# Two cross-attention and feed-forward layers on one core: values of a pair of head groups by seven products, and a written-out order at the end

## What is computed

```python
x = x + _L0_xattn_ref(_layernorm(x), ctx, mask, position_bias, ln_weight, w_q, w_k, w_v, w_out)
x = x + _L0_ffn_ref(_layernorm(x), ...)      # 512x512 base, low-rank part of 4 experts, softmax routing
x = x + _L1_xattn_ref(_layernorm(x), ctx, Wq, bq, Wk, bk)    # one head of width 512, values = ctx
x = x + _L1_ffn_ref(_layernorm(x), qweight, scale, zero_point, bias)   # 512x512, 6 bit codes

# _L0_xattn_ref
x = _rmsnorm(hidden_states, ln_weight)
h_q, h_k, h_v = x @ w_q.T, kv @ w_k.T, kv @ w_v.T            # each 1024 x 4096
score = softmax(where(mask, einsum(h_q, h_k) + position_bias))
out = einsum(score, h_v) @ w_out.T + hidden_states
```

## Time and profile before

| | |
|---|---|
| median of 3 runs | 980.95 us (980.33 to 982.57) |
| the profiled execution | 981.03 us, of which 979.2 us from first to last instruction |
| busy, of the span | PE 98%, PE weight loads 85%, DVE 62%, POOL 48%, ACT 40% |
| mean granted clock of TensorE | 0.993 of full |
| DMA | 169.6 MB, mean 173 GB/s |

### The profile page before, as it was taken

The page is one execution under the profiler, slowest core; times in us unless marked ns, Lnnn a source line. Parts: engine busy times, 40 slices in busy tenths (PEclk is TensorE's granted clock), DMA queues, the critical chain, the costliest instruction groups (busy, mean ns, idle before and its releaser), DMA issues.

```text
span 979.2 us, 16713 instructions
## 1 busy us (share of the span) xinstructions
PE 956.6 (98%) x5645; PEld 835.3 (85%) x5645; DVE 605.7 (62%) x1124; ACT 393.7 (40%) x1100; POOL 469.4 (48%) x527
## 2 busy tenths in 40 slices
PE   9999999999999999999999999999999999999995
PEld 7888888888888888888888888888888888777773
DVE  5664774656566666666565656565656568376774
ACT  5654444333434243433333333434333333424652
POOL 3550735464645545545546455555464612113676
PEclk9999999999999999999999999999999999899998
DMA  9223537747474756555555647474747442301001
GB/s 334 92 90 131 166 136 237 254 156 268 156 277 159 263 172 240 188 213 196 212 210 195 239 170 258 158 260 171 262 171 261 152 152 88 118 1 26 19 22 54
DMA packets 58185, 169.60 MB, mean 173 GB/s; under 512 B 5767, under 2 KB 7947, under 8 KB 57884
## 3 DMA queue, kind: packets, MB, share of 16 engines
q1 hardware_dynamic: 58140, 169.01, 49.1%
HBM read 158.51 MB, written 10.49 MB: 173 GB/s over the span
## 4 chain that ended last, share of the span: by engine, by line
PE 90%; DVE 4%; POOL 2%; ACT 2%; issue 1%; DMA 1%; SPq 0%; ACTq 0%; POOLq 0%; DVEq 0%
PE ps_q L326 6%; PE ps_q L328 6%; PE ps_q L327 6%; PE ps_v L328 6%; PE ps_v L326 6%; PE ps_v L327 6%; PE ps_o L326 6%; PE ps_o L328 6%; PE ps_o L327 6%; PE ps_s L1760 6%; PE ps_t L1787 6%; PE ps_k L326 6%; PE ps_k L328 5%; PE ps_k L327 5%; PE ps_t L1777 3%
## 5 line engine op out<-in xcount | busy, mean ns | idle before, releaser
L1206 DVE TENSOR_TENSOR acc<-ps_o,acc 128x512 f32<-128x512 f32 x128 | 87.9, 686 | 154.0 <-PE ps_o L328 154.0
L653 ACT ACTIVATE scores<-scores,neg_max 128x128 f32<-128x128 f32 x256 | 99.8, 391 | 197.0 <-DVE neg_max L1287 197.0
L326 PE MATMUL ps_v<-wv_hi,ct_hi 128*128 128x256 f32 x504 | 142.7, 283 | 0.0
L328 PE MATMUL ps_v<-wv_hi,ct_lo 128*128 128x256 f32 x504 | 142.7, 283 | 0.0
L327 PE MATMUL ps_v<-wv_lo,ct_hi 128*128 128x256 f32 x504 | 142.6, 283 | 0.0
L951 POOL TENSOR_TENSOR wq_lo<-raw_q,wq_hi 128x256 fp32r<-128x256 f32 x65 | 48.1, 740 | 159.8 <-ACT wq_hi L520 159.8
L326 PE MATMUL ps_o<-wo_hi,att_hi 128*128 128x512 f32 x256 | 106.2, 415 | 1.1 <-DVE att_lo L1194 1.1
L659 ACT COPY probs_t<-ps_t 128x512 f32<-128x512 f32 x64 | 37.7, 588 | 172.7 <-PE ps_t L1777 172.7
L328 PE MATMUL ps_o<-wo_hi,att_lo 128*128 128x512 f32 x256 | 100.3, 392 | 0.0
L327 PE MATMUL ps_o<-wo_lo,att_hi 128*128 128x512 f32 x256 | 99.9, 390 | 0.0
L326 PEld LDWEIGHTS ps_v<-wv_hi,ct_hi 128*128 128x128 f32 x504 | 96.5, 191 | 3.9 <-DVE vv L1160 0.9
(11 more groups left out here) (339 smaller groups left out, 2400.6 us busy)
## 6 DMA issues: line engine op xcount, KB each, us to landing
ring_hi<-scratch_x_t SPq DMA_DIRECT2D x39, 512.0 KB, 4.1
ring_lo<-scratch_x_t SPq DMA_DIRECT2D x39, 512.0 KB, 5.0
ring_hi<-scratch_c_t SPq DMA_DIRECT2D x39, 512.0 KB, 4.1
ring_lo<-scratch_c_t SPq DMA_DIRECT2D x39, 512.0 KB, 5.5
raw_v<-in_w_v SPq DMA_DIRECT2D x16, 512.0 KB, 5.6
raw_o<-in_w_o SPq DMA_DIRECT2D x16, 512.0 KB, 3.4
raw_q<-in_w_q SPq DMA_DIRECT2D x15, 512.0 KB, 6.0
raw_k<-in_w_k SPq DMA_DIRECT2D x15, 512.0 KB, 5.6
```

The lines of the kernel that those rows point to most:

```text
L326: pe.matmul(dst, hi_l, hi_r, start=first, stop=False)
L328: return pe.matmul(dst, lo_l, hi_r, start=False, stop=last)
L653: e = act.activation(probs[n][:, m, :], scores[n][:, m, :], ACT.Exp, bias=neg_max[:, n, m:m + 1], accum_out=row_sum[:, n, m:m + 1])
L1206: dve.tensor_tensor(acc[:, b, :], ps_o[:], acc[:, b, :], ALU.add).then_inc(o_added, 1)
```

## The change

The values of the groups 4 to 15 are made in pairs of groups by seven products as well: the four blocks are the token halves and the two groups of a pair. Each product has two halves (`unit_v`, 12 matmuls each, tokens of two batches), so a pair takes 14 of them in place of eight calls of `project_v` with 24. They stand in the steps of the turn before and of the pair's own. Groups 0 to 3 stay plain. POOL makes four weight sums for a pair, ACT and POOL split the seven weight blocks one by one, ACT copies the first product out, DVE adds the others. The raw weights lie in the unused half of two context blocks, which are saved to DRAM scratch and brought back at the end. The results of the odd group need two new buffers; the query and key sums use one buffer less (`mid` is halved, the intermediate lies in the place of the result) and their banks are exchanged. SP frees some ring blocks by the value products that read them last.

```diff
+            def unit_v(p, n, slot, b_hi, b_lo, chunk, col):
+                h = (n - 1) % 2
+                pe.wait_ge(wv_lo_s, v_weight(p, (n + 1) // 2))
+                if 2 <= n <= 3:
+                    pe.wait_ge(v_copy, 2 * p - 4 + n)
+                else:
+                    pe.wait_ge(v_out, v_count(p, (0, 0, 0, 0, 1, 2, 3, 4, 5, 6, 8, 10, 11, 12, 13)[n]))
+                for j in range(2):
+                    cols = slice(col + (2 * h + j) * P, col + (2 * h + j + 1) * P)
+                    for m in range(2):
+                        last = three(pe, ps_v[:, j * 2 * P:(j + 1) * 2 * P], b_hi[:, chunk + m, cols], b_lo[:, chunk + m, cols],
+                                     wv_hi[:, 2 * slot + m, :], wv_lo[:, 2 * slot + m, :], m == 0, m == 1)
+                last.then_inc(v_done, 1)
...
                 step_scores(s, c)
+                if c == 6 and coming:
+                    v_p6(i + 1, 1)
+                if c == 7 and coming:
+                    v_p7(i + 1, 1)
                 if c % 4 == 0:
                     q_p5(g)
+                if c == 4 and coming:
+                    v_p1(i + 1, 0)
...
-                step_v(s, c, g + (c % 4) // 2)
+                if c == 0 and own:
+                    v_p5(i, 0)
+                if c == 1:
+                    if own:
+                        v_p3(i, 0)
...
+                if c == 2:
+                    if own:
+                        v_p3(i, 1)
...
+                if c == 3:
+                    if own:
+                        v_p4(i, 0)
...
+                if c == 4:
+                    if coming:
+                        v_p1(i + 1, 1)
+                    else:
+                        v_p4(i, 1)
+                if c == 5 and coming:
+                    v_p2(i + 1, 1)
                 step_transpose(s, c)
                 output(s - 1, (c - 1) % LOOP_STEPS, None, (1,))
...
-                if c % 4 == 0:
+                if c % 4 == 0 and not (last and c == 4):
                     q_p3(g)
+                    if c == 0 and own:
+                        v_p5(i, 1)
+                    if c == 4:
+                        v_p2(i + 1, 0)
                     k_p3(g)
                 if c % 4 == 1 and more:
                     k_p1(G)
+                    if c == 5:
+                        v_p6(i + 1, 0)
                     k_p6(G)
...
+                    if c == 6:
+                        v_p7(i + 1, 0)
                     k_p2(G)
+                if c == 3 and own and not last:
+                    v_p4(i, 1)
```

(`own` is true from turn 2 on, `coming` in all turns but the last.) In the last turn the third query and key products move from step 4 to step 5. On POOL the sums:

```diff
+            def v_sums(p):
+                pool.wait_ge(odd_in, 32 * p - 16)
+                pool.tensor_tensor(v_even[0][:], v_even[0][:], v_odd[0][:], ALU.subtract).then_inc(v_sum_s, 1)
+                pool.wait_ge(v_done, v_count(p, 2))
+                pool.wait_ge(v_sum_s, 4 * p + 1)
+                pool.tensor_tensor(v_sum[:], v_odd[1][:], v_even[0][:], ALU.subtract).then_inc(v_sum_s, 1)
+                pool.wait_ge(v_sum_s, 4 * p + 2)
+                pool.tensor_tensor(v_even[1][:], v_even[1][:], v_sum[:], ALU.subtract).then_inc(v_sum_s, 1)
+                pool.tensor_tensor(v_odd[0][:], v_odd[0][:], v_odd[1][:], ALU.add).then_inc(v_sum_s, 1)
```

At the start of the last three layers DVE makes `a_lo` of batch 0 and the statistics of batch 1 ahead of the last four `r_batch` and the column made of them, which now stand at the end of turn 0 of `w`; statistics and inverse deviations of stage a run one batch further ahead. The turns 8 to 12 of `w` are replaced by one list per engine, and `c_hi` and `c_lo` get two buffers each. TensorE's list:

```diff
+            transpose(1, 6, b_full_s)
+            a_end(7)
+            b_scores(6)
+            b_attend(5)
+            transpose(2, 4, c_lo_s)
+            transpose(1, 7, b_full_s)
+            b_transpose(6)
+            c_product(3)
+            b_scores(7)
+            b_attend(6)
+            b_transpose(7)
+            transpose(2, 5, c_lo_s)
+            b_attend(7)
+            c_product(4)
+            transpose(2, 6, c_lo_s)
+            c_product(5)
+            transpose(2, 7, c_lo_s)
+            c_product(6)
+            c_product(7)
```

More of the change, by code:

```diff
@@ L219, in build @@
         b_full, _ = place("b_full", [P, NC, P], F32, at=at_qkv[1] + 6144)
[L220 to L221 removed]
+        c_hi = [place(f"c_hi{n}", [P, NC, P], F32R, at=(at_qkv[1] + 8192, at_qkv[0])[n])[0] for n in range(2)]
+        c_lo = [place(f"c_lo{n}", [P, NC, P], F32R, at=(at_qkv[1] + 10240, at_qkv[0] + 2048)[n])[0] for n in range(2)]
         b_probs, _ = place("b_probs", [P, P], F32, at=at_scores[0])
@@ L320, in w_part, with v_slot, v_count, v_weight @@
             return tile[:, head, 2 * half:2 * half + 2, :]
+        v_sum, _ = place("v_sum", [P, 2, 2 * P], F32, at=at_wv_lo + 4 * D)
+        def v_slot(tile, slot):
+            return tile[:, 2 * slot:2 * slot + 2, :]
+        def v_count(p, n):
+            return 14 * p - 12 + n
+        def v_weight(p, n):
+            return 7 * p - 10 + n
         block = stack.enter_context(nc.Block())
@@ L703, in step @@
                 more = not (last and c >= 4)
+                own = not (isinstance(i, int) and i == 1)
+                coming = not last
                 attention_high(s - 1)
@@ L837, in stage_c @@
                 act.wait_ge(n_t[2], b + 1)
-                wait_from(act, c_mm, b)
-                act.copy(c_hi[:], blocks(ps_k2)).then_inc(c_hi_s, 1)
+                wait_from(act, c_mm, b - 1)
+                if b == 1:
+                    act.wait_ge(base_lo_s, NC)
+                act.copy(c_hi[b % 2][:], blocks(ps_k2)).then_inc(c_hi_s, 1)
             normalise_end(0, 0)
-            for w in range(BATCH + 5):
+            for w in range(BATCH):
                 a, b, tc, c = w, w - 2, w - 4, w - 5
@@ L1041, in step @@
                     make_shift(s + 1, (c + 1) % LOOP_STEPS)
+                first = isinstance(i, int) and s == FIRST
+                own = not (isinstance(i, int) and i == 1)
+                coming = not last
                 if c % 4 == 0 and more:
-                    if isinstance(i, int) and s == FIRST:
+                    if first:
                         pool.wait_ge(wide_lo, 7)
@@ L1955, in step @@
                 more = not (last and c >= 4)
+                own = not (static and i == 1)
+                coming = not last
                 if not (static and s < 4 * PLAIN):
@@ L1971, in step @@
                     q_p6(G)
+                if last and c == 5:
+                    k_p3(g)
                 if c % 4 == 2:
```

687 lines of the change are left out of this document (480 added, 207 removed).

## The result

The changed kernel takes 969.61 us (median of 4 runs, 966.02 to 970.49) against 980.64 (979.29 to 982.57): ratio 0.9884, 95% interval 0.9866 to 0.9901. It is faster by 11.0 us where 20.0 were forecast, and lies above the range of 957 to 967.5. The profiled execution took 970.49 us with a span of 968.7, 10.5 less than the span before.

A forecast was written before the change was run, and what follows sets the result against it. TensorE was taken to bound the loop, hand-overs between engines the drain. The sum: 17.2 - 2.1 - 3.7 + 1.2 + 7.4 = 20.0 us gained, 981.0 - 20.0 = 961.0 us; range 957 to 967.5.

The forecast's parts named there:

- Part 1: Values of groups 4 to 15: seven products per pair save 144 matmuls of 0.12 us, gain 17.2 us.
- Part 2: Loop steps: softmax and accumulation get tight, stalls in step 0 (1.2 us) and step 5 (0.9), loss 2.1 us.
- rival of the shared place: Loop: DVE blocked by POOL in step 5, 2.7 us more, and a late ring block, 3.0; 964 to 967, chance 0.2.
- Part 3: Steps 4 and 5 of the last turn: TensorE waits for att_lo and transposes, loss 3.7 us of 4.3 saved.
- Part 5: Drain: new order and two buffers for c_hi and c_lo remove TensorE's c_lo waits, gain 7.4 us.
- Part 4: Start of the small last layers: first a_lo and second normed tile come earlier, net gain 1.2 us.
- slower rival: Loop: the softmax sets each of 48 steps, one more DVE operation ahead of each normalisation; 989.8 us, chance 0.03.

The follow-up runs named there:

- all_three: casts_behind plus, on POOL, step 0's key-weight sums after DVE's multiplication (turns 2 to 7) and turn 1's output-weight remainder before the value weights': 958.12 us.
- pool_waits: Changed kernel, but in step 4 of the last turn POOL makes the output weights' remainder only after DVE's four wk_lo: 967.77 us.
- rests_behind: Changed kernel, but in the last turn DVE makes the four wk_lo and four wq_lo later, behind step 5's accumulation and att_lo respectively: 962.40 us.
- old_drain: Changed kernel with the old order of the drain (turns 8 to 12 of w) on all engines, keeping both c_hi and c_lo buffers: 974.73 us.
- two_buffers: Kernel before the change, with two buffers for c_hi and c_lo and nothing else changed: 978.83 us, ratio 0.9999.
- casts_behind: rests_behind, and ACT makes the attention's cast of step 4 ahead of the four casts of wk: 961.95 us.

## Why the prediction was wrong, point by point

- **Part 1, 17.2 us by seven products: right.** 5645 matmuls became 5501, and where nothing stalls, a turn takes 98.5 instead of 101.33 (all_three).
- **Part 2, loop stalls of 2.1: right place, wrong size.** 1.9 more. Step 5 cost up to 0.1 a turn (0.15 booked); step 0 cost 0.5 to 0.8 (0.2 booked). I had let the multiplication end at 6.46; it ended at 6.63, since the small factor ahead of it was held up too (0.36 for 0.16), and then the transposes wait as well as the output. The rival of the shared place was right in kind and named the wrong step. No wait of TensorE for a ring block shows.
- **Part 3, the last turn: the step that failed.** Counted from the scores of step 4, I had the cast of the output weights begin at 8.5, the four casts end at 11.7, the attention's cast at 12.3 and DVE's rest at 13.0. Measured: 8.5, 11.7, 12.1 and 16.1. All of ACT is right; the rest comes 3 us late because wk_lo took 5.34, not 2.5. Part 2 had the very rule, and the order showed that POOL's wo_lo is let go by the cast just ahead of these four; I priced them at 0.61 each, which they do take in the kernel before, but there POOL stood still beside them. In pool_waits the rest is done at 13.2. The second miss is the clock, which this part put at nothing: it fell behind the pause of 4.5, and in rests_behind, with pauses of 1.3 to 1.8, it stayed. It is the larger one. The waits for att_lo are 6.5 in all, while the sum had 5.2 in this stretch (1.5 from before and the 3.7), because the 1.9 that it had for the transposes of step 5 did not come: TensorE was by then as late as they were. So about 1.4 of the 5.0 us are waits and 3.6 the clock. Part 5 looked at the clock; Part 3 did not.
- **Ahead of turn 2: 2.7 not in the sum.** 0.3 lie in the first 46 us, which differ by 1.1 between executions of the changed kernel and its variants, so they mean nothing. In turn 1 DVE's small operations on `targets` run beside POOL's sums (four in 1.44 us, 0.39 before), att_lo is late by 0.5, and wo_lo by 0.72. The other 1.2 are not traced to a wait. I had no term for the two straight-line turns, although the change moved 48 matmuls and POOL's work there.
- **Part 4: right in kind, too small.** 2.4 instead of 1.2. In this stretch TensorE waited 1.9 us for normed tiles before and none now, and I counted one wait of 1.00. Undoing the early a_lo and column gives 1.3 back in the trace.
- **Part 5: right.** 6.3 of 7.4, by the order, as old_drain and two_buffers show. The 1.1 left is POOL's chain at the end, 958.94 to 964.14, in which two operations are held up by DVE (1.82 and 1.80 instead of 1.28). It has three additions; the forecast said four, but its 3.9 us are three times 1.3.

The slower rival did not come near: of a turn's steps only 0 and, by up to 0.1, 5 are longer than their matmuls.

## What to carry to other kernels

A duration taken from a trace holds only with the neighbours it had there. When a change moves an operation of DVE with two SBUF inputs, look at what POOL does in its new place, and the other way round, before you put the old duration into the sum; a group of short ones behind one long POOL operation pays for what is left of it. And where a sum ends in a pause of TensorE of several us, price the clock behind it in every part, not only where the profile already shows a fall: here two pauses cost 6.5 us, most of which the sum had, and the clock 3.6 more, which it had not. In this drain the order did what buffers did not: two buffers alone gave 0. Before a gain is put down to an edit, set the stretches of the two traces against each other: one execution can have a fall of the clock that another one lacks, here for about 1.5 us.

## What the runs showed of the hardware that I had not expected

- The shared place works in both directions and down to the smallest operations: DVE 0.69 to 1.19 and 128x4 factors 0.16 to 0.36 beside POOL; POOL 0.74 to 1.18 and 1.28 to 1.82 beside DVE. Operations of DVE with one input are not all exempt: `neg_max` (TENSOR_SCALAR, 128x4) takes 0.17, but 1.19 beside POOL in casts_behind.
- The clock also falls without a long pause. At the start of the small layers it is at its lower level for some us in all thirteen traces, the kernel before among them (844 to 852 us in the changed kernel). Behind a pause of 0.68 TensorE does products of 32 and 4 columns there, without a further pause; what makes the clock fall was not tested. The fall is longer in seven of the traces than in the six others: from the wait for kb_row to the last a_lo the changed kernel and its variants with the same code there take 91.6 to 91.8 or 90.1 to 90.2 us, the kernel before 94.0 and two_buffers 92.6. The 2.4 of Part 4 compare long with long, and short with short gives the same.
- The spread between runs goes with the granted clock. One run of the changed kernel had a mean of 0.995 and took 966.02 us; the three others had 0.990 to 0.991 and took 969.04 to 970.49. The traces show two falls that come in one execution and not, or shorter, in another, each worth about 1.5 us; that they make the 3 us between these runs was not traced.
- A wait that the profile puts to "issue" was three times one for wo_lo, which only the second of the three matmuls reads: TensorE starts 0.1 us after POOL has made it (0.72, 3.54 and 0.54 us). The first went away with the order on POOL.
